# Gated cross-attention block on one core: the mask between the two steps of Q's rotation, sums of p one slot earlier, statistics by four

## The reference

```
def _layernorm(x, axis=-1, eps=1e-05):
    m = jnp.mean(x, axis=axis, keepdims=True)
    v = jnp.var(x, axis=axis, keepdims=True)
    return (x - m) / jnp.sqrt(v + eps)
...
        q = (query @ Wq).reshape(b, t, h, d)
        k = (key @ Wk).reshape(b, t, kv_h, d)
        v = (value @ Wv).reshape(b, t, kv_h, d)
        q = apply_rope(q)
        k = apply_rope(k)
...
        logits = logits * ATTN_MULT
        logits = MAX_ATTN_VAL * jnp.tanh(logits / MAX_ATTN_VAL)
        m = mask[:, :, None, :, :]
        logits = jnp.where(m, logits, -1e+30)
        weights = jax.nn.softmax(logits, axis=-1).astype(query.dtype)
        attn = jnp.einsum('bkgtT,bTkd->btkgd', weights, v)
        return attn @ Wo
...
    x = x + jnp.tanh(g_xattn[0]) * _L0_xattn_ref(_layernorm(x, axis=-1), ctx_4096, ctx_4096, ...)
    x = x + jnp.tanh(g_ffn[0]) * _L0_ffn_ref(_layernorm(x, axis=-1), ...)
```

## Time and profile before

| | us |
|---|---|
| median of 3 runs | 865.17 (864.29 to 866.2) |
| the profiled execution | 864.27 |
| its span | 862.5 |
| TensorE busy | 774.4 (90%) |
| VectorE busy | 641.0 (74%) |
| GpSimd busy | 602.7 (70%) |
| ScalarE busy | 423.7 (49%) |

### The profile page before, as it was taken

One profiled execution on the slowest core, in us unless ns is written; L12 is line 12 of the kernel. 1 busy time (PEld: TensorE's weight loads), 2 busy tenths in 40 slices (PEclk: granted clock), 3 DMA queues, 4 the chain that ended last, 5 costly groups with the idle time before them and its releaser, 6 DMA issues.

```text
span 862.5 us, 11913 instructions
## 1 busy us (share of the span) xinstructions
PE 774.4 (90%) x3650; PEld 622.0 (72%) x3650; DVE 641.0 (74%) x1168; ACT 423.7 (49%) x823; POOL 602.7 (70%) x437
## 2 busy tenths in 40 slices
...
DMA packets 57137, 41.70 MB, mean 48 GB/s; under 512 B 22938, under 2 KB 44442, under 8 KB 57082
## 3 DMA queue, kind: packets, MB, share of 16 engines
...
## 4 chain that ended last, share of the span: by engine, by line
POOL 51%; PE 25%; issue 15%; DVE 6%; ACT 1%; DMA 1%; POOLq 0%; SPq 0%; ACTq 0%; DVEq 0%
POOL aT_lo L559 10%; POOL q_rot L477 9%; POOL q_sin L472 9%; POOL probs L543 8%; POOL wo_lo L463 6%; POOL wq_lo L454 5%; PE bank_q L1146 2%; POOL wkv_lo L459 2%; PE bank_q L1147 2%; PE ps_o L52 2%; PE ps_o L54 2%; PE ps_o L53 2%; PE ps_s L52 1%; PE ps_s L53 1%; PE bank_kv L52 1%
## 5 line engine op out<-in xcount | busy, mean ns | idle before, releaser
L472 POOL TENSOR_TENSOR q_sin<-q_sin,q_tab 128x512 f32<-128x512 f32 x64 | 82.9, 1295 | 112.7 <-ACT q_sin L634 112.7
L52 PE MATMUL bank_q<-xT_hi,wq_hi 128*128 128x512 f32 x256 | 110.0, 430 | 6.2 <-ACT q_sin L634 4.8
L633 ACT COPY q_sin<-bank_q 64x512 f32<-64x512 f32 x64 | 37.3, 583 | 149.7 <-DVE q_cos L847 149.7
L52 PE MATMUL ps_o<-wo_hi,aT_hi 128*128 128x512 f32 x256 | 105.3, 411 | 2.3 <-POOL aT_lo L559 1.6
L54 PE MATMUL bank_q<-xT_hi,wq_lo 128*128 128x512 f32 x256 | 104.4, 408 | 0.0
L53 PE MATMUL bank_q<-xT_lo,wq_hi 128*128 128x512 f32 x256 | 104.1, 407 | 0.0
L559 POOL TENSOR_TENSOR aT_lo<-attn,aT_hi 128x512 fp32r<-128x512 f32 x64 | 101.5, 1586 | 2.4 <-ACT aT_hi L727 2.3
L54 PE MATMUL ps_o<-wo_hi,aT_lo 128*128 128x512 f32 x256 | 102.7, 401 | 0.0
L53 PE MATMUL ps_o<-wo_lo,aT_hi 128*128 128x512 f32 x256 | 102.5, 400 | 0.0
L477 POOL TENSOR_TENSOR q_rot<-q_cos,q_sin 128x512 f32<-128x512 f32 x64 | 83.1, 1299 | 5.0
L997 DVE TENSOR_TENSOR p_lo<-probs,p_hi 128x512 fp32r<-128x512 f32 x54 | 84.2, 1559 | 1.6 <-ACT p_hi L694 1.6
...
## 6 DMA issues: line engine op xcount, KB each, us to landing
...
packed<-in_down_q SPq DMA_DIRECT2D x10, 256.0 KB, 3.4
acc<-in_x SPq DMA_DIRECT2D x8, 256.0 KB, 5.9
wkv_raw<-in_Wk SPq DMA_DIRECT2D x8, 256.0 KB, 2.8
wkv_raw<-in_Wv SPq DMA_DIRECT2D x8, 256.0 KB, 3.2
```

Source lines behind the costliest of these rows:

```text
L52: nc.tensor.matmul(out, w_hi, m_hi, start=first, stop=False)
L472: nc.gpsimd.tensor_tensor(q_sin[:], q_sin[:], q_tab[:, 1, :].unsqueeze(1).to_broadcast([P, HALF, T]), ALU.mult).then_inc(q_sined, 1)
```

## The change

Five things are changed.

1. In slots 1 to 59 GpSimd applies the mask of s-1 between the two steps of Q's rotation, where it followed the second.
2. VectorE takes the partial sums of p of s-1 at the end of slot s, behind `attn` of s-2 and ahead of the addition to `acc`; before, it took those of s-2 in slot s, between `p_lo` and `cos_q`.
3. In slot 0 VectorE and ScalarE do V and K of the first sequence ahead of the fifth Q.
4. At the start the variances of four sequences together get epsilon and the power; the transposes of x use four PSUM banks; TensorE transposes four sequences, makes the first Q, then does the mask's transposes and those of the next sequences, each ahead of a product of Q.
5. x(2) and x(3) are loaded ahead of the first group's Wq, and ScalarE rounds the first part of Wq ahead of x.

```diff
-        x_banks = [ps_o[:], ps_pv[:]]
+        x_banks = [ps_o[:], ps_pv[:], ps_x[:], ps_tot[:]]
...
                 load_x(1)
+                load_x(2)
+                load_x(3)
                 for i in range(2):
                     ks = slice(2 * i, 2 * i + 2)
                     sp.dma_start(wq_raw[0][:, ks, :], wq_v[:, ks, 0:GC]).then_inc(ld_wq0[i], 16)
-                load_x(2)
-                load_x(3)
...
-                def invert_std(b):
-                    pool.wait_ge(var_done, b + 1)
-                    nc.gpsimd.tensor_tensor(rstd[:, b, :], rstd[:, b, :], minus_half[:], ALU.pow).then_inc(rstd_done, 1)
+                def invert_std(half):
+                    bs = slice(half * HALF, (half + 1) * HALF)
+                    pool.wait_ge(var_done, half + 1)
+                    nc.gpsimd.tensor_tensor(rstd[:, bs, :], rstd[:, bs, :], minus_half[:].unsqueeze(1).to_broadcast([P, HALF, 1]),
+                                            ALU.pow).then_inc(rstd_done, 1)
...
-                def rope(n):
+                def rope(n, mask_between=False):
...
                     pool.wait_ge(q_sined, n + 1)
                     pool.wait_ge(q_cosed, n + 1)
+                    if mask_between:
+                        apply_mask(n - AHEAD - 1)
                     wait(pool, qk_split, n - h - AHEAD)
                     nc.gpsimd.tensor_tensor(q_rot[:, half, h, :, :], q_cos[:], q_sin[:], ALU.add).then_inc(q_roped, 1)
...
                     if has_q_job(s):
-                        rope(s + AHEAD)
-                    if runs(s - 1) and s != SLOTS:
+                        rope(s + AHEAD, mask_between=s > 0)
+                    elif runs(s - 1) and s != SLOTS:
                         apply_mask(s - 1)
...
-                    if has_q_job(s):
+                    if 0 < s and has_q_job(s):
                         turn_q(s + AHEAD)
                     if runs(s):
                         act.wait_ge(kv_done, s + 1)
                         wait(act, pv_done, s - 3)
                         nc.scalar.copy(v_hi[:, s % 4, :], kv_bank(s)[:, 1, :]).then_inc(v_rounded, 1)
+                    if s == 0:
+                        turn_q(AHEAD)
...
-                def norm_moments(b):
-                    dve.wait_ge(ld_x[b], 16)
-                    nc.vector.bn_stats(stats[:, b, :], acc[:, b, :]).then_inc(stats_done, 1)
...
+                def norm_moments(half):
+                    for b in range(half * HALF, (half + 1) * HALF):
+                        dve.wait_ge(ld_x[b], 16)
+                        nc.vector.bn_stats(stats[:, b, :], acc[:, b, :]).then_inc(stats_done, 1)
...
-                    if runs(s - 2):
-                        dve.wait_ge(masked, s - 1)
-                        wait(dve, norm_done, s - 2)
-                        nc.vector.transpose(r_tot[:], probs[:, s % 2, :]).then_inc(p_turned, 1)
-                        dve.wait_ge(p_turned, s - 1)
-                        wait(dve, tot_done, s - 2)
-                        nc.vector.reduce_sum(partial[:], r_tot[:].rearrange("p (c e) -> p c e", e=32), AX_X).then_inc(p_summed, 1)
-                    if has_q_job(s):
+                    if 0 < s and has_q_job(s):
                         cos_q(s + AHEAD)
...
+                    if s == 0:
+                        cos_q(AHEAD)
...
                         nc.vector.tensor_tensor(attn[:], ps_pv[:], r_tot[:], ALU.mult).then_inc(norm_done, 1)
+                    if runs(s - 1):
+                        dve.wait_ge(masked, s)
+                        wait(dve, norm_done, s - 1)
+                        nc.vector.transpose(r_tot[:], probs[:, (s - 1) % 2, :]).then_inc(p_turned, 1)
+                        dve.wait_ge(p_turned, s)
+                        wait(dve, tot_done, s - 1)
+                        nc.vector.reduce_sum(partial[:], r_tot[:].rearrange("p (c e) -> p c e", e=32), AX_X).then_inc(p_summed, 1)
...
-                prep(0)
-                prep(1)
+                for b in range(HALF):
+                    prep(b)
+                make_q(0)
                 pe.wait_ge(mask_step, 6)
                 nc.tensor.transpose(ps_s[:, T:2 * T], live_rows[:], ident[:])
                 nc.tensor.transpose(ps_s[:, 0:T], keep[:], ident[:]).then_inc(keep_T, 1)
-                prep(2)
-                prep(3)
-                for n in range(AHEAD):
-                    make_q(n)
-                    prep(AHEAD + n)
+                prep(4)
+                prep(5)
+                make_q(1)
+                prep(6)
+                make_q(2)
+                prep(7)
+                make_q(3)
```

More of the change, by code:

```diff
@@ L634, in turn_q @@
                     nc.scalar.copy(q_sin[D // 2:D], q_banks[n % 2][0:D // 2]).then_inc(q_turned, 1)
-                for b in range(4):
+                round_w("wq", 0, 0)
+                for b in range(3):
                     prep_x(b)
-                    round_w("wq", 0, b)
+                    round_w("wq", 0, b + 1)
+                prep_x(3)
                 round_w("wkv", 0, 0)
-                prep_x(4)
                 round_w("wkv", 0, 1)
                 prep_ctx(0)
+                prep_x(4)
                 prep_x(5)
@@ L893, in _ @@
                 cos_q(1)
-                norm_moments(7)
                 norm_apply(7)
```

80 lines of the change are left out of this document (34 added, 46 removed).

## The result

The changed kernel takes 856.31 us (median of 4 runs, 855.1 to 857.64) beside 864.73 for the kernel before in the same session; the ratio is 0.9901, 95% interval 0.988 to 0.9922, so 8.6 us are gained (6.7 to 10.4). The forecast was 849, 16 us gained, range 839 to 861. The profiled execution took 855.1, span 853.3, against 864.27 and 862.5.

The account below looks back on a forecast made before the run. It took the period between ends of q_cos, which set off VectorE and GpSimd, as the bound, with 1.13 us of mutual waiting. Gains of 1 (middle), 10 (start) and 5.5 (tail) sum to 16.5: forecast 849 us, range 839 to 861.

Parts of the forecast that it names:

- The forecast's chain: Middle slots: qT_lo ends at 5.56 after the split, stretched aT_lo at 6.71, p_lo at 7.26; period 9.39 against 9.41.
- rival A: Middle slots: qT_lo misses the split's end and meets aT_lo, mean period 9.96, 28 us slower, total 877; chance 0.10.
- The steady slots: About 51 middle slots in the new order: 0.02 us gained in each, 1 us in all, bounds -3 and +3.
- the new wait costs 0.07: GpSimd, middle slots: the mask waits for exp and starts at 1.21 after v_lo, where q_sin allows 1.14.
- the margin of 0.26: Middle slots: qT_lo arrives on VectorE at 4.75 after v_lo, only 0.26 before GpSimd's weight split ends at 5.01.
- The start: Before the middle slots: earlier fifth Q and K first in slot 0; gain 10 us, bounds 6 and 12.
- x(3) landed at 6 to 7, the four statistics and the power by 8: Start: when the last of the first four x loads arrives and their joint variance work is done, in us.
- the first product at 15: Start: four rounds of normalising, transposing and rounding at an estimated 1.7 each put Q's first product at 15 us.
- The tail: Slots 60 to 63: sums made a slot earlier end TensorE's idling before ps_tot; gain 5.5 us, bounds 2 and 9.
- Rival B: Middle slots: p_lo isn't held by aT_lo, TensorE bounds at about 8.95, 23 us faster, total 826; chance 0.08.

Follow-up runs that it names:

- experiment 2: The changed kernel with the mask put back behind q_rot, the partial sums left at their new place: 877.89 us, ratio 1.0176 to the kernel before.
- experiment 10: The changed kernel with GpSimd's aT_lo made on only 32 of 512 columns in slots 8 to 55: 823.96 us, ratio 0.9508 to the kernel before.
- experiment 5: The changed kernel with ScalarE's tanh, without exp, moved ahead of the turn of Q: 853.95 us, ratio 0.987 to the kernel before.
- experiment 1: The changed kernel with mask and partial sums back at their old places, so the start's change alone: 858.39 us, ratio 0.9936 to the kernel before.
- experiment 7: The changed kernel with the mask at its old place and the sums at theirs up to slot 60, new from there: 849.75 us, ratio 0.9825.
- experiment 3: The changed kernel with ScalarE's tanh and exp both moved ahead of the turn of Q: 868.96 us, ratio 1.0054 to the kernel before.
- experiment 4: The changed kernel with q_cos moved ahead of p_lo in VectorE's slot: 813.58 us, ratio 0.9414 to the kernel before.
- experiment 11: The changed kernel with q_cos ahead of p_lo up to slot 56, then old mask place, sums old until slot 60 and early from 60: 813.62 us, ratio 0.9413.
- experiment 6: The changed kernel with the partial sums back between p_lo and q_cos, the mask left at its new place: 868.69 us, ratio 1.0032.
- experiment 8: The kernel with only the start's change, mask and sums at old places, with q_cos moved ahead of p_lo: 865.88 us, ratio 1.0014 to the kernel before.

## Why the prediction was right in direction and too high in size

- **The method.** The reading of the earlier trace rows, two engines that hold each other's instructions, carried every steady slot. The forecast's chain (qT_lo to 0.55 behind the split, aT_lo stretched, p_lo to 0.55 behind aT_lo) is in the trace after with each term 0.08 to 0.10 later, rival A's chain is in experiment 2 to 0.05, and p_lo is freed in experiment 10. The forecast cites the Trainium skill (SBUF — State Buffer, "Who interferes with whom") for this: a VectorE instruction with two SBUF inputs and a GpSimd instruction that reads SBUF contend, and one blocks until the other is done. By that rule, experiment 10 agrees: p_lo takes 0.68 where no GpSimd instruction is under way.
- **The steady slots: the step that failed** is "with 0.08 for the signal (the gap between q_sin and q_rot) the mask starts at 1.21". From exp to the mask it was 0.17. Everything behind it hangs on that start one to one (experiment 5: 0.17 sooner, 0.15 to 0.16 off the period). So "the new wait costs 0.07" should have been 0.16, and there was 0.02 in hand to cover it. I had given the whole middle bounds of ±3 for signals of 0.04 to 0.08; the wait alone took 4.6 us. Pricing the gap by one between ScalarE and GpSimd wouldn't have helped, since q_sin shows 0.08 for that too. What the kernel before doesn't show anywhere in its middle is a mask whose two waits are met within 0.1 us of each other. The other 1.8 of the middle are three slots in which one instruction starts 0.3 to 0.35 later than elsewhere.
- **Rival A** was priced right: the forecast has 877 for it, and experiment 2, where qT_lo comes too late in every slot, measures 877.89. In the changed kernel the margin of 0.26 (0.28 in the trace after, both sides of it later by 0.1) failed in one slot of 51, by the late transpose.
- **The start**: 10 forecast. Behind the first q_cos 8.2 were forecast, and the profiles gave 8.5, 7.8 and 6.4 (the changed kernel, experiments 1 and 7). "x(3) landed at 6 to 7, the four statistics and the power by 8" and "the first product at 15" didn't hold even in the best profile: x(3) was there in time, but the power on four columns takes 1.03 (0.55 for one) and ended at 9.02, and the first product stood at 16.71. The first q_cos was at 24.6 in the median of twelve profiles where I had 22.3; in three of them VectorE also stood for the last of the four transfers. By the times the start alone is worth 5.5 (3.7 to 7.3).
- **The tail**: 5.5 forecast, 6.2 in the profile. That was luck, two errors that cancel: the tail's order gives 8.7 by itself in the profile of experiment 7 (9.6 by the ratios), and the sums ahead of the unpacking, of which I had priced only slot 60, take 2.3 back in two slots.
- **Rival B**: its cause was real (experiment 10), its floor wrong. I took TensorE's 95.44% of the earlier trace rows as 8.95 a slot (the product is 8.98); at 8.69 it is 99.86% busy. TensorE's matmuls of 512 columns start 0.23 apart when nothing stands between them and are listed with 0.39 each, so the last one ahead of a wait covers 0.16 of the wait. By the matmuls' start times 0.71 of a slot of the kernel before is waiting, which leaves 8.69.
- **What I missed** is that p_lo needn't stand ahead of q_cos at all. The forecast says that the end of q_cos sets both engines off, and that p_lo's wait is in its way, and didn't draw the conclusion.

Left open: why the transpose of probs is 0.35 late once, between the seventh v_lo and the eighth. It is so in all six kernels in which the sums have their new place and don't stand for the mask there (the changed one and experiments 3, 4, 5, 10 and 11), at the same instruction. Open too is why the mask is about 0.3 late in two slots, the same two in the five kernels in which it waits for exp (the changed one and experiments 4, 6, 10 and 11). Transfers of instructions lie within 2 us of two of these places in the changed kernel, which is no proof.

## What to carry to other kernels

Find the event that sets the next round off (here the end of q_cos) and put behind it whatever doesn't lead to it, the instructions that get held by another engine most of all. A move that pays nothing in one order can be what makes another pay: the mask's and the sums' places lose 6.5 us in the middle here, and without them the 43 us of q_cos's place are not to be had (experiment 8).

Multiply a small term by the slots before you call it small, and give its bounds for the case that you haven't seen: a new second wait that is met just behind the first cost 0.17 here, where either wait alone costs 0.08. When several transfers' waits are joined into one, it is the last transfer's, with its spread (three of twelve profiles here stood for it, for up to 2.1 us).

## What the runs showed of the chip

- A VectorE subtraction of two tiles in SBUF takes 0.68 with GpSimd idle; with a GpSimd instruction under way it ends 0.55 behind that one's end (0.54 to 0.56 in nearly all slots of the kernel before and the changed one), up to 1.77 in all. GpSimd's next instruction, which had started beside it, takes 1.75 instead of 1.30 for 512 columns, and 0.70 for 32 (experiment 10); no run has the 32 columns unheld.
- From the end of a ScalarE instruction to a GpSimd one that waits for it: 0.08 (q_sin, all 61 of the kernel before that wait); from one GpSimd instruction to the next that waits for it: 0.08; from exp to the mask, which the end of q_sin allows at nearly the same moment: 0.17. On VectorE 0.04 from the transpose to the reduction, but 0.11 from attn to the transpose, which the program also has wait for the mask, even where the mask ended 0.4 earlier (experiment 5).
- The profile's TensorE share can stand at 95% with over 7% of the period still to be had (9.41 to 8.69).
- GpSimd's power takes 0.55 on 128x1 in the kernel before and 1.03 on 128x4 in the changed one: four together are cheaper in sum, but each of the four then waits for all.
